# Summing the messages over destinations: loads of four columns, eight split slots, one-hots on GpSimd

## The chip, the cores and the metric

The kernel runs on one core of a Trainium2 chip. A core has TensorE (matrix products, into PSUM), VectorE (DVE), ScalarE (ACT), GpSimd (POOL) and SyncE (SP), which here issues most of the DMAs. The engines run side by side and wait for one another through semaphores. The metric is the device time of one execution in microseconds (us), as the median of several runs; lower is better.

## The reference

A stack of graph layers on 1250 nodes with 768 features and 20000 edges sorted by destination: two GCN layers, a relational layer (34 relations) with a GCN behind it, two attention layers and one more GCN, each block with a layer norm and a residual. The change touches the end of the relational layer:

```python
seg = edge_type * n + dst
agg = jax.ops.segment_sum(x[src], seg, num_segments=N_REL * n)
cnt = jax.ops.segment_sum(ones, seg, num_segments=N_REL * n)
mean = agg.reshape(N_REL, n, -1) / jnp.maximum(cnt, 1.0).reshape(N_REL, n, 1)
h1 = jnp.einsum('rni,rio->no', mean, W_rel) + x @ W_root + b_rgcn
xw = h1 @ W_gcn
```

`dst` is int(1250 u²) for uniform u, so the first nodes have many more edges than the last ones.

## The kernel before

The kernel computes the mean over relations edge by edge. In the relation stage each edge's source row, multiplied by its relation's weights and by the reciprocal of its count, is scattered by GpSimd to `messages` in DRAM, in the order of the edges, which is the order of destinations. 128 edges make a column: there are 157, padded to 160.

The stage after it, which the program calls the sum, computes h1 for ten tiles of 128 nodes. For a tile, TensorE turns its rows of h (six transposes, `turn`, L1240) and multiplies them by the root weights (36 matmuls, `products`, L1249), into two PSUM banks. On top of that it adds the tile's columns of messages: a column is multiplied by a one-hot matrix (edge to node of the tile), 128 x 128, made by VectorE at L1205 from the edge's destination. Columns go in groups of four, `QUAD`; a column at a border of tiles is taken for both.

Products are split for accuracy: a float32 operand is written as a rounded high part and a low rest. So a column passes through four engines. SP loads it into one of four slots `w_raw[:, b]` (L502) as soon as VectorE is done with that slot (`Q.ylow`). ScalarE copies it to the high part, `y_part[:, 0, k]` in the memory of `xw` (L817), when the load has landed and TensorE is done with this slot of the group before (`Q.ymm`). VectorE makes the one-hot (L1205) and subtracts the high part from the message for the low part (L1207). TensorE multiplies the high and the low part, each in two halves of 384 features: four matmuls (L1417).

The order of each engine's instructions is written out by hand in `sum_tile` of each engine. VectorE: copy the next tile's rows (L1199), all columns of this tile, the low parts of the next tile's turned rows (`turn_low`, L856), then, when TensorE is done with the tile's last column, the bias and PSUM into `h_act` (L1212). ScalarE: the columns, then the high parts of the next tile's turned rows (L808). TensorE: the next tile's turning, the root products of this tile, its columns. SP: the columns' loads. The bounds of the loops are read from small tables (`bounds`, L358 and L359; `quads`, L361 to L364), since they depend on the data.

GpSimd issues the gathers and scatters of the relation stage (L599, L604, L636), each behind a small copy of its addresses (L595, L630), and has nothing to do in the sum. Before the relation stage it reads back the edge records (L590) and starts the first gathers, for which VectorE waits at L1166.

Semaphores `pre.*` order the preparation at the start of the kernel, in which the unused rows of `messages` are zeroed as well (L400 to L405).

Of the kernel before, what the change touches and what calls it, by code (L numbers as in the profile page):

```python
# [5 lines left out]
P = 128  # L6
# [8 lines left out]
ds = bass.ds  # L15
# [5 lines left out]
QUAD = 4  # L21
RING = 4

class EdgeSems:

    def __init__(self, sem):
# [6 lines left out]
        self.turned = sem("pre_turned")  # L35
        self.extremes = sem("pre_extremes")
        self.extremes_turned = sem("pre_extremes_turned")
        self.best = sem("pre_best")
        self.row = sem("pre_row")
        self.tot = sem("pre_tot")  # L40
        self.prefix = sem("pre_prefix")
# [58 lines left out]
class SumSems:  # L100

    def __init__(self, sem):
        self.copied = sem("sum_copied")
        self.turned = sem("sum_turned")
        self.high = sem("sum_high")
        self.low = sem("sum_low")
        self.mm = sem("sum_mm")
        self.yhigh = sem("sum_yhigh")
        self.ylow = sem("sum_ylow")  # L110
        self.ymm = sem("sum_ymm")
        self.ofree = sem("sum_ofree")
# [47 lines left out]
def gnn_stack(nc, A, out):  # L160
# [33 lines left out]
    messages = nc.dram_tensor("messages", (YROWS, D), F32).ap()  # L194
    inv_table = nc.dram_tensor("inv_table", (NP * NR, 1), F32).ap()

    with ExitStack() as ctx:
# [11 lines left out]
        w_raw = sb("w_raw", [P, KB, D], F32)  # L209
        agg_w = sb("agg_w", [P, 2, NT, P], F32R)[:]  # L210
        h_t = sb("h_t", [P, 2, KB, P], F32R)
        rows = sb("rows", [P, 4, D], F32)
# [34 lines left out]
        y_part = xw[:, :, 0:QUAD, 0:D]  # L247
        h_flat = h_act[:].rearrange("p t d -> p (t d)")
        rows_flat = rows[:].rearrange("p a d -> p (a d)")
        raw_flat = w_raw[:].rearrange("p k d -> p (k d)")  # L250
        n_eq = NR * ECP
        rec_in = rows_flat[:, D:D + 3 * RIN].bitcast(I32).rearrange("p (c w) -> p c w", w=3)
# [6 lines left out]
        oh = h_flat[:, n_eq:n_eq + ohw].bitcast(BF16).rearrange("p (u n) -> p u n", u=2)  # L259
        adj_t = rows_flat[:, 0:NP]  # L260
# [60 lines left out]
        x_copy, zeroed = sem("x_copy"), sem("zeroed")  # L321
# [17 lines left out]
        y_land = [sem(f"y_land{b}") for b in range(QUAD)]  # L339
# [6 lines left out]
        QMAX = NT * (ECP // QUAD)  # L346
# [32 lines left out]

        def score_row(t, which):  # L380

            return ps_flat[:, ds(t % 2 * (6 * 512) + which * 512, P)]
# [3 lines left out]
        def _(sp):  # L386
# [10 lines left out]
            sp.dma_start(x_state[0:N, :], x).then_inc(x_copy, 16)  # L397
            sp.wait_ge(pre.zeros, 1)
            sp.dma_start(x_state[N:NP, :], zero_rows[0:NP - N, 0, :]).then_inc(zeroed, 16)
            at = E  # L400
            while at < ECP * P:
                n = min(ECP * P - at, 3 * 80)
                sp.dma_start(messages[at:at + n, :].rearrange("(p r) d -> p r d", r=3), zero_rows[0:n // 3, :, :])\
                  .then_inc(zeroed, 16)
                at += n  # L405
# [60 lines left out]
            sp.wait_ge(x_copy, 16)  # L466
            sp.wait_ge(zeroed, 16 * 3)
# [65 lines left out]
        def _(pool):  # L533
# [111 lines left out]
            pool.sem_inc(R.stored, 1)  # L645

        @block.scalar
        def _(act):
# [185 lines left out]
        def _(dve):  # L835
# [178 lines left out]
            dve.wait_ge(pre.turned, 1)  # L1014
# [13 lines left out]
            dve.sem_inc(pre.extremes, 1)  # L1028
            dve.wait_ge(pre.extremes_turned, 1)
# [419 lines left out]
```

## Time and profile before

| | |
|---|---|
| time, median of 3 runs | 3085.62 us (3083.73 to 3091.12) |
| profiled execution, its own time | 3085.96 us |
| its span in the trace | 3084.0 us |
| mean granted TensorE clock | 0.939 |
| busy: PE, DVE, ACT, POOL | 85%, 52%, 37%, 28% |

The time of an execution is its span and about 2 us around it. In the profile, idle time stands with what ended it ("releaser"), and the busy time of TensorE is that of a pipeline whose ends are modelled. PEclk is the granted clock, 1.00 for 2.4 GHz and 0.50 for 1.2 GHz.

### The profile page before, as it was taken

How to read it: one execution, taken by the hardware profiler on the slowest of the kernel's cores; microseconds unless marked ns; L12 is line 12 of the kernel's file. 1: busy time of each engine (PE TensorE's matmuls, PEld its weight loads, DVE VectorE, ACT ScalarE, POOL GpSimd, SP SyncE). 2: the span in 40 equal slices, each digit the busy share in tenths (PEclk: the TensorE clock that was granted, in tenths of full speed). 3: DMA queues.
4: the chain of work that ended last, by engine and by line, in shares of the span. 5: the costliest groups of instructions: out<-in, count | busy, mean ns of one | idle time of the engine just before them, and what ended most of it. 6: DMA issues, size and time to landing. Idle time of an engine off the chain costs nothing.

```text
span 3084.0 us, 52263 instructions
## 1 busy us (share of the span) xinstructions
PE 2621.4 (85%) x14502; PEld 2425.3 (79%) x14503; DVE 1604.0 (52%) x3028; ACT 1126.3 (37%) x1925; POOL 859.8 (28%) x1207
## 2 busy tenths in 40 slices
PE   0666388976999999999999999677778898987899
PEld 0222188976999999999999999556668887987799
DVE  7765543354344333443334433477764577577734
ACT  0011323232444444444444444355433235446521
POOL 1666610002555555555555555100000000000000
PEclk9987689998999999999999999889989998998999
DMA  3000110124445544555544554577660201001102
GB/s 108 1 1 1 44 47 0 45 86 169 175 174 182 196 174 174 174 188 190 174 174 172 195 188 143 184 239 228 207 199 21 77 25 36 10 13 69 51 21 91
DMA packets 116601, 358.08 MB, mean 116 GB/s; under 512 B 23709, under 2 KB 24177, under 8 KB 116337
## 3 DMA queue, kind: packets, MB, share of 16 engines
q1 hardware_dynamic: 78097, 220.40, 21.2%
q0 software_dynamic: 38464, 137.17, 12.8%
q8 instruction: 23, 0.38, 0.0%
q14 instruction: 17, 0.14, 0.0%
HBM read 267.97 MB, written 93.37 MB: 117 GB/s over the span
## 4 chain that ended last, share of the span: by engine, by line
PE 72%; DVE 11%; issue 5%; ACT 5%; DMA 4%; DVEq 2%; POOL 0%; ACTq 0%; SPq 0%; POOLq 0%
PE ps L1249 50%; PE ps L1304 12%; PE ps L1240 5%; PE ps L1356 4%; DMA w_raw<-messages 3%; DVE xw L1207 1%; PE ps L1417 1%; ACT xw L817 1%; DVE h_act L1115 1%; ACT rows L721 1%; DVE h_act L927 1%; DVEq L1113 1%; PE ps L1362 1%; DVE w_a L850 1%; DVE rows L981 1%
## 5 line engine op out<-in xcount | busy, mean ns | idle before, releaser
L1249 PE MATMUL ps<-w_a,h_t 128*128 128x384 f32 x5580 | 1032.3, 342 | 2.4 <-DVE h_t L856 2.1
L1249 PEld LDWEIGHTS ps<-w_a,h_t 128*128 128x128 f32 x5580 | 982.3, 192 | 6.9 <-DVE h_t L856 4.6
L1304 PE MATMUL ps<-xw,agg_w 128*128 128x384 f32 x2800 | 524.5, 350 | 78.8 <-DVE agg_w L952 47.2
L1304 PEld LDWEIGHTS ps<-xw,agg_w 128*128 128x128 f32 x2800 | 512.6, 197 | 87.7 <-issue 77.1
L1249 PE MATMUL ps<-xw,h_t 128*128 128x384 f32 x3132 | 577.4, 341 | 0.0
L1155 DVE TENSOR_TENSOR h_t<-ps,h_t 128x256 fp32r<-128x256 f32 x516 | 218.7, 424 | 678.5 <-ACT h_t L784 482.3
L1249 PEld LDWEIGHTS ps<-xw,h_t 128*128 128x128 f32 x3132 | 549.0, 188 | 0.0
L784 ACT ACTIVATE h_t<-ps 128x256 fp32r<-128x256 f32 x516 | 198.2, 384 | 677.2 <-PE ps L1249 472.0
L1240 PE MATMUL ps<-ident,rows 128*128 128x128 f32 x1458 | 206.8, 280 | 129.7 <-DVE rows L863 71.2
L636 POOL DMA_INDIRECT messages<-rows,rec_stage x172 | 199.9, 1162 | 354.1 <-ACT rows L778 354.1
L1240 PEld LDWEIGHTS ps<-ident,rows 128*128 128x128 f32 x1458 | 176.4, 144 | 146.3 <-issue 86.1
L599 POOL DMA_INDIRECT h_act<-h_table,rec_stage x175 | 188.7, 1078 | 147.1 <-POOL rec_stage L595 119.4
L1417 PE MATMUL ps<-xw,agg_w 128*128 128x384 f32 x736 | 178.2, 381 | 54.5 <-DVE xw L1207 50.0
L817 ACT ACTIVATE xw<-w_raw 128x768 fp32r<-128x768 f32 x184 | 152.6, 843 | 167.3 <-DMA w_raw<-messages 91.2
L1417 PEld LDWEIGHTS ps<-xw,agg_w 128*128 128x128 f32 x736 | 134.7, 206 | 95.9 <-DVE xw L1207 94.5
L1356 PE MATMUL ps<-h_act 128*128 128x512 bf16 x552 | 151.0, 393 | 63.1 <-DVE h_act L1115 53.6
L604 POOL DMA_INDIRECT w_at<-inv_table,rec_stage x175 | 182.9, 1045 | 61.4 <-issue 61.4
L1207 DVE TENSOR_TENSOR xw<-w_raw,xw 128x768 fp32r<-128x768 f32 x184 | 176.0, 957 | 44.4 <-ACT xw L817 43.7
L575 POOL DMA_INDIRECT records<-rec_stage x157 | 158.4, 1009 | 128.4 <-POOL rec_stage L571 121.7
L856 DVE TENSOR_TENSOR h_t<-ps,h_t 128x256 fp32r<-128x256 f32 x213 | 86.9, 423 | 185.6 <-ACT h_t L664 184.2
L1356 PEld LDWEIGHTS ps<-h_act 128*128 128x128 bf16 x552 | 43.4, 105 | 173.8 <-DVE h_act L1115 133.2
L664 ACT ACTIVATE h_t<-ps 128x256 fp32r<-128x256 f32 x183 | 70.2, 385 | 295.8 <-PE ps L1249 206.1
(183 smaller groups left out, 2188.8 us busy)
## 6 DMA issues: line engine op xcount, KB each, us to landing
w_raw<-in_L_gnn_W_rel SPq DMA_DIRECT2D x68, 1152.0 KB
w_raw<-messages SPq DMA_DIRECT2D x184, 384.0 KB, 3.8
rows<-x_state SPq DMA_DIRECT2D x50, 384.0 KB, 3.0
w_raw<-in_L_gnn_W SPq DMA_DIRECT2D x10, 1152.0 KB
x_state<-rows SPq DMA_DIRECT2D x30, 384.0 KB, 2.3
h_table<-h_act SPq DMA_DIRECT2D x10, 384.0 KB, 2.4
x_state<-in_x SPq DMA_DIRECT2D x1, 3750.0 KB, 14.2
out<-rows SPq DMA_DIRECT2D x9, 384.0 KB
```

What stands on the lines that cost most here:

```text
L599: pool.indirect_dma_start(out=x_ring[:, k, :], out_offset=None, in_=h_table, in_offset=bass.IndirectOffsetOnAxis(gather_at[:, k, 0:1], 0)) ...
L604: pool.indirect_dma_start(out=w_at[:, k:k + 1], out_offset=None, in_=inv_table, in_offset=bass.IndirectOffsetOnAxis(gather_at[:, k, 1:2], ...
L636: pool.indirect_dma_start(out=messages, out_offset=bass.IndirectOffsetOnAxis(scatter_at[:, k, :], 0), in_=rows[:, 2 + u, :], in_offset=Non ...
L784: act.activation(h_t[:, 0, 2 * g:2 * g + 2, :], turn_group(g).rearrange("p (k n) -> p k n", k=2), ACT.Copy)\
L817: act.activation(y_part[:, 0, k, :], w_raw[:, k, :], ACT.Copy).then_inc(Q.yhigh, 1)
L1155: dve.tensor_tensor(h_t[:, 1, 2 * g:2 * g + 2, :], turn_group(g).rearrange("p (k n) -> p k n", k=2), h_t[:, 0, 2 * g:2 * g + 2, :].bitcast ...
L1207: dve.tensor_tensor(y_part[:, 1, k, :], w_raw[:, k, :], y_part[:, 0, k, :].bitcast(F32), ALU.subtract)\
L1240: ins = pe.transpose(turn_out(k), tile[:, k * P:(k + 1) * P], ident[:])
L1249: ins = pe.matmul(acc(h), h_t[:, a, k, :], w[:, b, k, h * HF:(h + 1) * HF], start=(k == 0 and a == 0 and b == 0), stop=(stop and k == KB - ...
L1304: ins = pe.matmul(ps[:, 2 + 2 * u + h, 0:wide], agg_w[:, a, b, :], xw[:, c, b, h * HF:h * HF + wide], start=first, stop=last, skip_group_c ...
L1356: ins = pe.matmul(ps_flat[:, lo:hi], oh[:, k % 2, 0:P], oh[:, k % 2, P + lo:P + hi], start=False, stop=True, skip_group_check=True)
L1417: ins = pe.matmul(rel_acc(t)(h), agg_w[:, 0, k, :], y_part[:, b, k, h * HF:(h + 1) * HF], start=False, stop=True, skip_group_check=True)
```

## The change

- The message slots grow from four to eight. `w_raw` (six rows of 768) and `rows` (four) become parts of one memory, `land`; its first eight rows are the ring for the loads. One DMA of 1536 KB brings a whole group of four columns, and two groups can be under way.
- SP loops over pairs of groups. The first column of each group comes from a new table, `quad_col`, that VectorE computes in `quad_columns` once, before the relation stage. A group's load is issued when VectorE has split the group two before it. Then SP waits until the group before the new one has landed and counts `Q.yready` up, for which ScalarE waits.
- The slots of the split parts grow from four to eight (`LAND`). Their addresses, and those of the ring, now depend on the group's number.
- The one-hots are made by GpSimd, in four slots as before: for every tile a copy of 128 node numbers, for every column a copy of the column's destinations, and the comparison.
- The turned rows go through `rows[:, 2]` in place of `rows[:, 0]`.
- Several semaphores of the preparation are put together, and the zeroing of `messages` is laid out differently.

```diff
-            with sp.Fori(0, NT) as t:
-                q0, q1, c0 = quads(sp, t)
-                with sp.Fori(q0, q1) as q:
-                    for b in range(QUAD):
-                        j = column(c0, q, q0, b)
-                        sp.wait_ge(Q.ylow, q * QUAD + b + 1)
-                        sp.dma_start(w_raw[:, b, :], messages[ds(j * P, P), :])\
-                          .then_inc(y_land[b], 16)
+            pairs = sp.value_load(ctl_half[0:1, 1:2], min_val=1, max_val=QMAX // 2)
+            with sp.Fori(0, pairs) as i:
+                for u in range(2):
+                    j = sp.value_load(quad_col[0:1, ds(2 * i + u, 1)], min_val=0, max_val=ECP - QUAD)
+                    sp.wait_ge(Q.ylow, i * LAND + (QUAD * u + QUAD))
+                    sp.dma_start(y_ring[:, QUAD * u:QUAD * (u + 1), :], message_rows[:, ds(j, QUAD), :]).then_inc(y_land[u], 16)
+                    sp.wait_ge(y_land[1 - u], i * 16 + 16 * u)
+                    sp.sem_inc(Q.yready, 1)
+            sp.wait_ge(y_land[1], pairs * 16)
+            sp.sem_inc(Q.yready, 1)
...
+            with pool.Fori(0, NT) as t:
+                q0, q1, c0 = quads(pool, t)
+                pool.wait_ge(Q.hot, q0 * QUAD)
+                pool.tensor_copy(hot_iota, iota_n[:, ds(t * P, P)]).then_inc(pre.rec_copy, 1)
+                with pool.Fori(q0, q1) as q:
+                    for k in range(QUAD):
+                        j = column(c0, q, q0, k)
+                        pool.tensor_copy(hot_node[:, k:k + 1], edge[:, 1, ds(j, 1)]).then_inc(pre.rec_copy, 1)
+                        pool.wait_ge(Q.ymm, q * QUAD + (k + 1 + QUAD))
+                        pool.sem_inc(turn_taken, 1)
+                        pool.wait_ge(pre.rec_copy, q * QUAD + t + (EC + k + 2))
+                        pool.sem_inc(turn_taken, 1)
+                        pool.tensor_scalar(agg_w[:, 0, k, :], hot_iota, hot_node[:, k:k + 1], None, ALU.is_equal)\
+                            .then_inc(Q.hot, 1)
...
-                        act.wait_ge(y_land[k], q * 16 + 16)
+                        act.wait_ge(Q.yready, q + 2)
                         act.wait_ge(Q.ymm, q * QUAD + (k + 1))
-                        act.activation(y_part[:, 0, k, :], w_raw[:, k, :], ACT.Copy).then_inc(Q.yhigh, 1)
+                        act.activation(part(0, q, k), landed(q, k), ACT.Copy).then_inc(Q.yhigh, 1)
...
+            def quad_columns():
+
+                q_first, q_base, q_delta = att[0:1, 0, :], att[0:1, 1, :], seg_max[0:1, 0, :]
+                dve.wait_ge(R.addr, 1)
...
+                for t in range(NT):
+                    link(dve.tensor_scalar(quad_step, iota_n[0:1, 0:QMAX], q_first[:, t:t + 1], q_delta[:, t:t + 1],
+                                           ALU.is_ge, ALU.mult))
+                    link(dve.tensor_tensor(quad_acc, quad_acc, quad_step, ALU.add))
...
-                        dve.wait_ge(Q.ymm, q * QUAD + (k + 1))
-                        dve.tensor_scalar(agg_w[:, 0, k, :], iota_n[:, ds(t * P, P)], edge[:, 1, ds(j, 1)], None, ALU.is_equal)
                         dve.wait_ge(Q.yhigh, q * QUAD + (k + 1))
-                        dve.tensor_tensor(y_part[:, 1, k, :], w_raw[:, k, :], y_part[:, 0, k, :].bitcast(F32), ALU.subtract)\
+                        dve.tensor_tensor(part(1, q, k), landed(q, k), part(0, q, k).bitcast(F32), ALU.subtract)\
                            .then_inc(Q.ylow, 1)
...
                     for k in range(QUAD):
-                        pe.wait_ge(Q.ylow, q * QUAD + (k + 1 + QUAD))
+                        pe.wait_ge(Q.hot, q * QUAD + (k + 1))
+                        pe.wait_ge(Q.ylow, q * QUAD + (k + 1 + LAND))
                         for b in range(2):
                             for h in range(2):
-                                ins = pe.matmul(rel_acc(t)(h), agg_w[:, 0, k, :], y_part[:, b, k, h * HF:(h + 1) * HF],
+                                ins = pe.matmul(rel_acc(t)(h), agg_w[:, 0, k, :], part(b, q, k)[:, h * HF:(h + 1) * HF],
                                                 start=False, stop=True, skip_group_check=True)
```

`part(a, q, k)` and `landed(q, k)` are the slots `q % 2 * QUAD + k` of `y_part` and of the ring; `link` makes VectorE wait for its own last instruction.

## Rows read from the trace of the kernel before

**Rows 1.** TensorE's message matmuls by tile: stretch, us, PE busy (xcount), PEclk, DMA share, GB/s

```profile
1967.00:2052.70 85.70, 54.38 (x208) 0.87 0.75 238
2052.70:2094.50 41.80, 23.31 (x96) 0.92 0.71 221
...
2130.00:2158.90 28.90, 15.52 (x64) 0.94 0.70 227
...
2188.30:2210.00 21.70, 10.54 (x48) 1.00 0.65 219
...
2231.80:2256.50 24.70, 11.35 (x48) 0.85 0.64 204
2256.50:2282.30 25.80, 12.22 (x48) 0.76 0.58 178
2282.30:2296.10 13.80, 6.66 (x32) 0.96 0.40 128
sum 329.10, PE 178.24; mean PE 17.82
```

**Rows 2.** Groups of instructions in the sum, 1965 to 2297 us

```profile
L1207 DVE TENSOR_TENSOR xw<-w_raw,xw 128x768 fp32r<-128x768 f32 x184 | 176.0, 957 | 44.4 <-ACT xw L817 43.7
L817 ACT ACTIVATE xw<-w_raw 128x768 fp32r<-128x768 f32 x184 | 152.6, 843 | 167.3 <-DMA w_raw<-messages 91.2 <-PE ps L1417 70.8 <-issue 1.9
...
L1205 DVE TENSOR_SCALAR agg_w<-iota_n,edge 128x128 fp32r x176 | 49.7, 282 | 46.6 <-PE ps L1417 29.8 <-issue 16.8
```

**Rows 3.** The chain of waits inside tile 0: start us, us, what

```profile
2015.28 3.83 DMA w_raw<-messages
2019.21 0.85 ACT xw L817
2020.09 0.97 DVE xw L1207
...
2039.50 4.42 DMA w_raw<-messages
```

**Rows 4.** Timeline behind the sum: two loads of 1152 KB, and ScalarE waiting

```profile
2297.08 0.92 SPq L411 DMA_DIRECT2D w_raw<-in_L_gnn_W_gcn  x2
...
2302.50 2.12 ACT L655 ACTIVATE w_a<-w_raw 128x2304 fp32r<-128x2304 f32 x1 [8.63 <-DMA w_raw<-in_L_gnn_W_gcn]
...
2305.38 2.12 ACT L655 ACTIVATE w_a<-w_raw 128x2304 fp32r<-128x2304 f32 x1 [0.75 <-DMA w_raw<-in_L_gnn_W_gcn]
```

**Rows 5.** Timeline at the border of tiles 2 and 3

```profile
2126.70 0.96 DVE L1207 TENSOR_TENSOR xw<-w_raw,xw 128x768 fp32r<-128x768 f32 x1
...
2129.04 0.96 DVE L1212 TENSOR_TENSOR h_act<-ps,rows 128x768 f32 x1 [0.37 <-PE ps L1417]
...
2131.15 6.49 PE L1249 MATMUL ps<-w_a,h_t 128*128 128x384 f32 x36
2132.29 0.29 DVE L1205 TENSOR_SCALAR agg_w<-iota_n,edge 128x128 fp32r x1 [1.83 <-issue]
```

**Rows 6.** Register instructions of ScalarE at L778: ns min/median/max, first and last start

```profile
L778 ACTq FUSED_REGOPS  x344: 98/100/141, 752.9 to 1947.0; - x172
```

**Rows 7.** GpSimd's first instruction that waits for its own engine

```profile
6.17 0.29 POOL L554 TENSOR_SCALAR_AFFINE_SELECT ident<-ident 128x128 f32<-128x128 f32 x1 [0.16 <-POOL rows L551]
```

**Rows 8.** GpSimd and VectorE by line, ns min/median/max, over the whole kernel

```profile
L595 POOL COPY rec_stage<-rows x175: 185/190/934, 732.9 to 1944.3; 128x2 int32 x172, 128x2 int32<-128x2 int32 x3
...
L636 POOL DMA_INDIRECT messages<-rows,rec_stage x172: 1014/1014/1770, 755.1 to 1949.0; - x172
...
L1163 DVE TENSOR_TENSOR xw<-w_raw,xw x102: 946/956/1035, 749.3 to 1872.8; 128x768 fp32r<-128x768 f32 x102
...
L1114 DVE TENSOR_SCALAR h_act<-iota_n,edge x184: 539/549/789, 77.2 to 349.3; 128x1280 bf16<-128x1280 uint16 x184
```

**Rows 9.** Timeline ahead of the relation stage

```profile
725.89 0.11 POOL L589 MEMSET rows<- 128x10 int32 x1 [320.95 <-DMA h_table<-h_act]
...
740.90 0.56 DVE L1167 COPY rows<-h_act 128x768 f32<-128x768 f32 x1 [18.50 <-POOLq L612]
```

More of the change, by code:

```diff
@@ L21 @@
 QUAD = 4
+LAND = 2 * QUAD
 RING = 4
@@ L34, in __init__ @@
         self.floats = sem("pre_floats")
[L35 to L41, printed above, removed]
+        self.pe_step = sem("pre_pe_step")
+        self.dve_step = sem("pre_dve_step")
         self.tile_ctl = sem("pre_tile_ctl")
@@ L108, in __init__ @@
         self.mm = sem("sum_mm")
+        self.yready = sem("sum_yready")
+        self.hot = sem("sum_hot")
         self.yhigh = sem("sum_yhigh")
@@ L208, in gnn_stack @@
         w_a = sb("w_a", [P, 2, KB, D], F32R)
-        w_raw = sb("w_raw", [P, KB, D], F32)
+        land = sb("land", [P, KB + 4, D], F32)
+        w_raw, rows = land[:, 0:KB, :], land[:, KB:KB + 4, :]
+        y_ring = land[:, 0:LAND, :]
         agg_w = sb("agg_w", [P, 2, NT, P], F32R)[:]
         h_t = sb("h_t", [P, 2, KB, P], F32R)
-        rows = sb("rows", [P, 4, D], F32)
         bias = rows[:, 3, :]
@@ L338, in gnn_stack @@
         Q = SumSems(sem)
-        y_land = [sem(f"y_land{b}") for b in range(QUAD)]
+        y_land = [sem(f"y_land{b}") for b in range(2)]
         block = ctx.enter_context(nc.Block())
@@ L378, in tile_rows, with landed, part @@
             return ap[:, ds(t, 1), :].rearrange("p a d -> p (a d)")
+        def landed(q, k):
+            return y_ring[:, ds(q % 2 * QUAD + k, 1), :].rearrange("p a d -> p (a d)")
+        def part(a, q, k):
+            return y_part[:, a, ds(q % 2 * QUAD + k, 1), :].rearrange("p a d -> p (a d)")
         def score_row(t, which):
@@ L1027, in _ @@
                 link(ins)
-            dve.sem_inc(pre.extremes, 1)
-            dve.wait_ge(pre.extremes_turned, 1)
-            dve.tensor_reduce(small[0:2 * NT, 1, 0:1], ps[0:2 * NT, 2, 0:P], AX.X, ALU.max).then_inc(pre.best, 1)
-            dve.wait_ge(pre.row, 1)
+            dve.sem_inc(pre.dve_step, 1)
+            dve.wait_ge(pre.pe_step, 2)
+            dve.tensor_reduce(small[0:2 * NT, 1, 0:1], ps[0:2 * NT, 2, 0:P], AX.X, ALU.max).then_inc(pre.dve_step, 1)
+            dve.wait_ge(pre.pe_step, 3)
             up, down = ps[0:1, 3, 0:NT], ps[0:1, 3, NT:2 * NT]
@@ L1165, in rel_split @@
                         ins.then_inc(w_low, 1)
+            quad_columns()
             dve.wait_ge(R.ready, 1)
@@ L1190, in _ @@
             dve.sem_inc(Q.ofree, 2)
-            dve.sem_inc(Q.ylow, QUAD)
+            dve.sem_inc(Q.ylow, LAND)
             dve.wait_ge(R.h_back, 16)
-            dve.tensor_copy(rows[:, 0, :], tile_rows(h_act, 0)).then_inc(Q.copied, 1)
+            dve.tensor_copy(rows[:, 2, :], tile_rows(h_act, 0)).then_inc(Q.copied, 1)
             turn_low(Q, 0)
@@ L1328, in _ @@
                 ins = pe.transpose(ps[:, 1, a * 32:(a + 1) * 32], float_b[:, a, :], ident[0:32, 0:32])
-            ins.then_inc(pre.turned, 1)
-            pe.wait_ge(pre.extremes, 1)
-            pe.transpose(ps[0:2 * NT, 2, 0:P], small[:, 0, 0:2 * NT], ident[:]).then_inc(pre.extremes_turned, 1)
-            pe.wait_ge(pre.best, 1)
+            ins.then_inc(pre.pe_step, 1)
+            pe.wait_ge(pre.dve_step, 1)
+            pe.transpose(ps[0:2 * NT, 2, 0:P], small[:, 0, 0:2 * NT], ident[:]).then_inc(pre.pe_step, 1)
+            pe.wait_ge(pre.dve_step, 2)
             pe.matmul(ps[0:1, 3, 0:2 * NT], small[0:2 * NT, 1, 0:1], ident[0:2 * NT, 0:2 * NT], start=True, stop=True)\
-              .then_inc(pre.row, 1)
-            pe.wait_ge(pre.tot, 1)
+              .then_inc(pre.pe_step, 1)
+            pe.wait_ge(pre.dve_step, 3)
             own = small[:, 3, 0:NR]
             pe.matmul(ps[:, 4, 0:NR], before[:], own, start=True, stop=True, skip_group_check=True)
-            pe.matmul(ps[:, 4, 64:64 + NR], ones[:], own, start=True, stop=True, skip_group_check=True).then_inc(pre.prefix, 1)
+            pe.matmul(ps[:, 4, 64:64 + NR], ones[:], own, start=True, stop=True, skip_group_check=True).then_inc(pre.pe_step, 1)
             cuts = [(0, 512), (512, 1024), (1024, NP + NR)]
@@ L1397, in _ @@
             pe.wait_ge(w_low, 2 * (w_no["root"] + 1))
-            pe.sem_inc(Q.ymm, QUAD)
+            pe.sem_inc(Q.ymm, LAND)
             pe.wait_ge(Q.copied, 1)
-            turn(Q, rows[:, 0, :])
+            turn(Q, rows[:, 2, :])
             def sum_tile(t, more):
@@ L1405, in sum_tile @@
                     pe.wait_ge(Q.copied, t + 2)
-                    turn(Q, rows[:, 0, :])
+                    turn(Q, rows[:, 2, :])
                 pe.wait_ge(Q.ofree, t + 1)
```

55 lines of the change are left out of this document (33 added, 22 removed).

## The prediction

> **What bounds the kernel now.** I read the page's slices first (the sum lies near 2000 to 2300 us), then the busy time by tile, then the groups of the stage, then the chain of waits, then single borders in the timeline. The sum takes 329.1 us for ten tiles [rows 1]. Sixteen matmuls are a group of four columns, so the tiles have 13, 6, 5, 4, 4, 3, 3, 3, 3 and 2 groups, 46 in all. TensorE's message matmuls are busy for 178 of these 329 us, VectorE's subtractions for 176, ScalarE's copies for 153: no engine fills the stage. ScalarE waits 91 us for loads and 71 us for TensorE [rows 2], and VectorE in turn for ScalarE.
>
> The chain says why. Inside a tile it goes round: load 3.8 us, ScalarE's copy 0.85, VectorE's subtraction 0.97, and 0.25 until the slot's next load starts. Between 2015.28 and 2039.50 there are four such rounds, 6.05 us each, one per group [rows 3]. Four loads are in flight, and what limits is the time from free slot to filled slot, not the bytes. Between tiles a second limit shows: from VectorE's last subtraction (end at 2127.66) it takes 1.4 us to the bias addition, 3.5 to the root products, which last 6.5, and 4.6 to VectorE's next one-hot [rows 5]. During the products only four columns can be split ahead; then ScalarE stands still until TensorE frees a slot, and the loads behind it too. Tiles with three groups took 21.7 us at full clock [rows 1], which is 3.5 us over three rounds.
>
> **The change part by part.** The sum is made against the profiled execution, 3085.96 us (span 3084.0 and 1.96 around it), 0.3 above the median of the runs.
>
> *The load of a group.* No message load of 1536 KB is in the trace, and I take its time from the two weight loads of 1152 KB: issued at 2297.08 and within 0.9 us, the first landed at about 2302.4 and the second at about 2305.3, where ScalarE began [rows 4]. So 1152 KB cost 2.9 us more, and 2.4 us are fixed: 1536 KB land in 2.4 + 3.9 = 6.3 us. I take 6.05 to 6.3. The ends: 5.3 us, the time of the 1152 KB, and 7.2, if the other group still has a fifth of its bytes to move (0.9 us).
>
> *The new round.* A slot's group is issued 0.25 us after its predecessor is drained, lands 6.05 later, waits 0.1 for SP, and is then split: first copy 0.85, four subtractions of which three start 0.9 apart and the last takes 0.96, 3.65 in all [rows 2, 3]. New register work for the ring's addresses stands between the wait and the instruction on both engines; two such instructions took 0.1 us each in the one place that has them [rows 6], so 0.2 on ScalarE and 0.2 on VectorE (ends 0 and 0.3 each). Sum 11.3 us for two groups, 5.65 a group. There is a second loop: SP counts a group ready only after it has issued the next load, and for that waits until VectorE has drained the group before. So ScalarE can't start a group while VectorE still splits the last one. That loop is 0.25 + 0.45 (issue) + 0.2 (two signals) + 0.2 + 0.85 + 0.2 + 3.65 = 5.8 us a group. The longer one holds: 5.8 against 6.05. Without the register work it would be 5.4. Thus inside long tiles the doubled ring brings only 0.25 us a group, since it buys depth and gives most of it back by coarse signals.
>
> *The border of tiles.* Here the change helps more. After the last subtraction VectorE goes through the low parts, bias, copy and the reading of its bounds as before; one bound less and no one-hot bring its first subtraction from 4.8 (0.2 behind the one-hot) to about 4.0 us after the drain [rows 5]. Then one group ends at 7.8 us and each further one 5.8 later: T(n) = 2.0 + 5.8 n, while root products run beside the first two. For n = 3 that is 19.4 against 21.7, for n = 4 25.2 against 28.9, for n = 6 36.8 against 41.8 [rows 1]. Over tiles 1 to 9, 33 groups: 18 + 191.4 = 209.4, and 0.9 less since the last ends in the bias addition, against 243.4: 34.9 us. Of these, 7.1 lie in the two tiles of 24.7 and 25.8 us, whose granted clock was 0.85 and 0.76 [rows 1]; I leave them to the clock, so 27.8. Tile 0: first subtraction 0.6 earlier, twelve rounds 0.2 shorter, 2.9 us.
>
> *The one-hots.* 184 instructions of 0.282 us, 52 us, leave VectorE [rows 2]; most lay in its waits for ScalarE, and the part on the path is in T(n). That hides behind 5.8 in the steady rounds. It doesn't quite after the root products: only four one-hots exist, the fifth can start when TensorE frees the first at 10.8 us, and the last of n groups is ready at 11.1 + 1.4 (4n - 5). For n = 3 with its column on TensorE 21.6 us, against 20.4 by the splits. About 1 us for each of nine tiles: 9 us lost.
>
> *Smaller ones.* TensorE's matmuls now take their address from a register. In the steady rounds TensorE has time; behind the root products, where eight columns wait, a tenth of a us per column costs 0.8 us a tile at most: 2 us (0 to 8). `quad_columns` is some 20 linked instructions on 400 elements, between 0.28 (128 elements) and 0.96 (768) each, so 0.5, and ten small ones: 10 + 2 to 14 us. It starts when GpSimd's memset is done at 726.0, and VectorE is needed at 740.9 [rows 9]: covered by 15 us, with little to spare. But GpSimd's address copies and gathers beside it can be held by up to 0.75 us each, and the relation stage starts behind them. 2 us (0 to 6). The merged semaphores, the zeroing and the moved rows: same work, in places where other loads or waits cover it; 0.
>
> *Sum.* 27.8 + 2.9 - 9 - 2 - 2 = 17.7 us less: 3085.96 - 17.7 = 3068.
>
> The shared port is where a rule speaks against this change. The holds above are GpSimd behind VectorE. The Trainium skill, "SBUF — State Buffer", section "SBUF: two separate sides", says that VectorE and GpSimd share a port pair by an exclusive lock, which an instruction of GpSimd or one of VectorE with two SBUF inputs holds to its end while the other is blocked fully; each subtraction is of that kind. By that rule, the trace agrees on the one side (0.19 to 0.93), and shows less on the other: subtractions of the relation stage went from 0.956 to 1.035 at most.
>
> **The rivals.**
>
> *B, GpSimd and VectorE take turns, slower.* Place: columns within a group. If every GpSimd instruction that meets a subtraction also delays the next one, a group grows. The row for it is VectorE's comparison beside GpSimd's copies, 0.549 in the median and up to 0.789 [rows 8], 0.2 to 0.24 longer; against it stands the 1.035. Four such delays a group are 0.8 us: rounds of 6.6 instead of 5.8, 36 us on 45 rounds, so 3068 + 36 = 3104. The same follows from a slow column on GpSimd alone: a tile can't be shorter than 11 + 4c(n - 1), ten tiles 110 + 144c. That reaches 329 us at c = 1.53; with one full hold of 0.75 a column, c = 1.65, it is 348, and with the 2 of `quad_columns` the kernel takes about 3107. It decides from c = 1.53, close above my 1.4.
>
> *C, the border is worth all that it seems.* c near 1, the clock stays up since TensorE's gaps are shorter, no register cost: 9 + 7 + 2 come back, and 0.2 us on each of 45 rounds, 9: 3068 - 27 = 3041. For it: tiles at clock 1.00 were 3 to 4 us shorter. Against: nothing in the trace shows address registers at no cost.
>
> *D, the coarse load eats the gain.* The group lands 7.2 us after its issue, and the first loop is 12.4 us, 6.2 a group: 0.4 more on 45 rounds, 18 us, 3068 + 18 = 3086, no change. The change would then do what it says and bring nothing, being bound by landing as now.
>
> **How the numbers follow.** My forecast 0.46, B 0.21, C 0.20, D 0.13. The range goes from somewhat below C to B: lower end, full removal of all uncertain costs with the load at 5.3 us, about 3038; upper 3104. The likeliest case has 3058 to 3078 for its own. A difference of 0.3% is 9.3 us, about what a measurement tells from no change: faster below 3076.4. Faster: most of my case (0.42) and C (0.20), 0.62. Same: the rest of mine and most of D, 0.15. Slower: B and a little of D, 0.23.
>
> **What would show it.** In the profile after: the sum at some 310 us, the chain inside tile 0 through ScalarE, VectorE's four subtractions and SP, with no or little landing time, rounds of 5.8; ScalarE's idle time ended by SP and not by TensorE; tiles of three groups near 20 to 21 us; TensorE waiting now and then for GpSimd's comparison, which takes about 0.3 us alone and up to 1 us behind a subtraction. The subtractions stay at 0.96. VectorE's first copy of the relation stage at 741 to 744. The forecast is wrong if subtractions grow to 1.1 or more, if TensorE mostly waits for GpSimd (B), if the load's landing ends ScalarE's waits in every group (D), or if the sum falls below 290 (C).

## The result, and the profile after

| | before | after |
|---|---|---|
| median | 3085.19 us (20 runs, 3080.15 to 3094.67) | 3091.03 us (20 runs, 3086.18 to 3099.54) |
| profiled execution, its own time | 3085.96 | 3087.34 |
| its span; granted clock | 3084.0; 0.939 | 3085.6; 0.936 |
| the sum, ten tiles | 329.1 | 325.4 |

The ratio of after to before is 1.0017, with a 95% interval of 1.0009 to 1.0025: some 5 us slower, a small loss, but clear of 1 (the medians themselves lie 5.8 us apart). All ratios here are of fast executions, without one of the kernel before of 3244.61 us and one of 5266.12 us of the kernel with fine loads and four copies. Forecast were 3068 us and a sum of some 309 (329.1 less 27.8 and 2.9, plus 9 and 2). The sum gave back 3.7 us instead of 20.

TensorE's message matmuls by tile (stretch, us, PE busy, PEclk, DMA share, GB/s), for tiles 0, 1, 3 and 5, against [rows 1]:

```profile
1971.30:2056.20 84.90, 54.03 (x208) 0.85 0.75 257
2056.20:2096.80 40.60, 23.87 (x96) 0.92 0.66 225
...
2131.70:2160.90 29.20, 14.97 (x64) 0.88 0.64 219
...
2189.70:2213.50 23.80, 10.99 (x48) 0.86 0.57 201
```

Tile 0 and tile 1 are about 1 us shorter (85.7 and 41.8 before), the tile of four groups is as long as it was (28.9), and the two tiles of three groups that had taken 21.7 and 21.8 grew to 23.8. The two later ones, which had a low clock before (24.7 and 25.8 us at 0.85 and 0.76), took 23.4 and 22.0 at 0.93. The groups of the sum, 1965 to 2297 us (busy, mean ns, idle time and what ended it), against [rows 2]:

```profile
L1461 PE MATMUL ps<-xw,agg_w 128*128 x736 | 180.3, 392 | 54.4 <-POOL agg_w L670 54.2 <-issue 0.2
L670 POOL TENSOR_SCALAR agg_w<-rec_out 128x128 fp32r<-128x128 uint16 x182 | 170.8, 939 | 79.7 <-PE ps L1461 44.0 <-POOL rec_out L665 35.7
L1250 DVE TENSOR_TENSOR xw<-land,xw x184 | 168.9, 979 | 92.6 <-ACT xw L843 83.3 <-issue 9.4
...
L843 ACT ACTIVATE xw<-land x184 | 140.2, 833 | 169.7 <-SPq L512 143.3 <-PE ps L1461 23.1 <-SPq L514 3.2
...
L665 POOL COPY rec_out<-edge 128x1 f32 x181 | 69.1, 382 | 0.5
```

Read the idle columns. The loads no longer end ScalarE's waits (91.2 us before), nor does TensorE much (70.8 before, 23.1 now); SP's signal L512 does. TensorE's own idle time is still 54 us, but now all of it ends in GpSimd's comparison L670, where 50 of 54.5 us ended in VectorE's subtractions in the kernel before:

```profile
L1417 PE MATMUL ps<-xw,agg_w 128*128 128x384 f32 x736 | 178.2, 381 | 54.5 <-DVE xw L1207 50.0
```

It shows most at the end of a tile. From VectorE's last subtraction to the bias addition it was 1.1 to 2.4 us in the ten tiles before, 16.9 in all; now it is 4.3 to 5.7, 50.9 in all, since TensorE still waits for one-hots. VectorE's wait for TensorE ahead of the bias addition (us, times, longest), before and after:

```profile
DVE h_act L1212 <- PE ps L1417: 7.6, 10, 1.4
...
DVE h_act L1255 <- PE ps L1461: 41.9, 10, 4.7
```

So the sum without these stretches did get shorter, by some 38 us (3.7 and 34), as much as the 34.9 and 2.9 that the forecast had for the borders and for tile 0 at whatever clock, and TensorE's wait for one-hots took almost all of it. GpSimd's and VectorE's instructions by line (ns min/median/max, first and last start), and from the same view of L510 the landing of a group's load:

```profile
L670 POOL TENSOR_SCALAR agg_w<-rec_out x184: 602/605/2092, 1962.5 to 2294.8; 128x128 fp32r<-128x128 uint16 x184
...
L665 POOL COPY rec_out<-edge x184: 180/186/989, 1961.8 to 2294.4; 128x1 f32 x184
...
L1250 DVE TENSOR_TENSOR xw<-land,xw x184: 943/955/1085, 1973.9 to 2291.3; - x184
...
DMA to landing us min/median/max: 6.3/6.5/10.4
```

The comparison takes 0.605 us by itself and 0.94 in the mean, the copy 0.186 and 0.38. VectorE's subtractions beside them have a median of 0.955, as before, a mean of 0.979 (0.957 before), and never more than 1.085. One group in the timeline (start, us, engine and line, idle time before):

```profile
2009.94 3.66 DVE L1250 TENSOR_TENSOR xw<-land,xw  x4 [2.33 <-ACT xw L843]
...
2010.30 1.86 POOL L670 TENSOR_SCALAR agg_w<-rec_out 128x128 fp32r<-128x128 uint16 x1 [0.20 <-POOL rec_out L665]
2012.11 0.67 POOL L665 COPY rec_out<-edge 128x1 f32 x1
...
2012.98 1.09 POOL L670 TENSOR_SCALAR agg_w<-rec_out 128x128 fp32r<-128x128 uint16 x1 [0.20 <-POOL rec_out L665]
...
2014.03 0.18 POOL L665 COPY rec_out<-edge 128x1 f32 x1
...
2014.41 0.60 POOL L670 TENSOR_SCALAR agg_w<-rec_out 128x128 fp32r<-128x128 uint16 x1 [0.20 <-POOL rec_out L665]
...
2015.35 0.60 POOL L670 TENSOR_SCALAR agg_w<-rec_out 128x128 fp32r<-128x128 uint16 x1 [0.20 <-POOL rec_out L665]
```

VectorE's four subtractions fill 2009.94 to 2013.60. GpSimd's instructions that start ahead of their end take 1.86, 0.67 and 1.09 us; those behind it 0.18 and 0.60. Undisturbed, a column costs GpSimd 2015.35 less 2014.41, 0.94 us: 0.60 for the comparison, 0.18 for the copy, 0.20 for the wait, less a slight overlap. The chain of waits inside tile 0 is GpSimd's as well (start, us, what):

```profile
2018.91 0.68 POOL rec_out L665
...
2025.13 0.68 POOL rec_out L665
...
2031.13 0.68 POOL rec_out L665
...
2037.21 0.68 POOL rec_out L665
```

The same held copy comes back every 6.1 us, one round of four columns, where [rows 3] had a round of 6.05 through load, ScalarE and VectorE. TensorE's bound has moved to another engine, and the round is as long as before. VectorE's own rounds beside it, which hang on SP's signal, are 6.05 us in the mean of tile 0, so the two are nearly equal inside a tile, and GpSimd's lag comes out at the tile's end.

### The profile page after: what moved, and what is told of

Read it like the earlier page. It is cut to its first block, busy times and chain, and to the rows that moved or that the text cites. A ratio compares the mean times of both kernels' runs of the same rounds, so it can differ in the third digit from the quotient of the medians.

```text
span 3085.6 us, 54594 instructions
## 1 busy us (share of the span) xinstructions
PE 2620.4 (85%) x14502; PEld 2431.2 (79%) x14503; DVE 1577.5 (51%) x2874; ACT 1114.0 (36%) x1925; POOL 1097.6 (36%) x1586
## 4 chain that ended last, share of the span: by engine, by line
PE 72%; DVE 10%; issue 8%; ACT 4%; POOL 3%; DVEq 2%; DMA 1%; POOLq 1%; ACTq 0%; SPq 0%
PE ps L1292 48%; PE ps L1347 11%; PE ps L1283 5%; PE ps L1399 4%; PE ps L1461 2%; POOL rec_out L665 1%; POOL agg_w L670 1%; DVE h_act L1141 1%; DVE h_act L953 1%; ACT land L747 1%; DVEq L1139 1%; PE ps L1405 1%; DVE w_a L876 1%; DVE land L1007 1%; DVE land L966 1%
## 5 line engine op out<-in xcount | busy, mean ns | idle before, releaser
L1347 PE MATMUL ps<-xw,agg_w 128*128 128x384 f32 x2800 | 526.2, 350 | 78.1 <-DVE agg_w L978 46.7
L1347 PEld LDWEIGHTS ps<-xw,agg_w 128*128 128x128 f32 x2800 | 514.0, 197 | 87.3 <-issue 77.6
L810 ACT ACTIVATE h_t<-ps 128x256 fp32r<-128x256 f32 x516 | 198.3, 384 | 675.9 <-PE ps L1292 477.5
L647 POOL DMA_INDIRECT messages<-land,rec_stage x172 | 200.1, 1163 | 353.2 <-ACT land L804 353.2
L1283 PE MATMUL ps<-ident,land 128*128 128x128 f32 x1458 | 207.2, 280 | 133.5 <-DVE land L889 71.5
L1283 PEld LDWEIGHTS ps<-ident,land 128*128 128x128 f32 x1458 | 176.7, 144 | 150.2 <-issue 89.6
L1461 PE MATMUL ps<-xw,agg_w 128*128 x736 | 180.3, 392 | 54.4 <-POOL agg_w L670 54.2
L1250 DVE TENSOR_TENSOR xw<-land,xw x184 | 168.9, 979 | 92.6 <-ACT xw L843 83.3
L1461 PEld LDWEIGHTS ps<-xw,agg_w 128*128 128x128 f32 x736 | 144.5, 217 | 88.5 <-issue 88.3
L843 ACT ACTIVATE xw<-land x184 | 140.2, 833 | 169.7 <-SPq L512 143.3
L670 POOL TENSOR_SCALAR agg_w<-rec_out 128x128 fp32r<-128x128 uint16 x184 | 172.0, 935 | 80.5 <-PE ps L1461 44.0
```

The costliest lines, as they stand in the source:

```text
L647: pool.indirect_dma_start(out=messages, out_offset=bass.IndirectOffsetOnAxis(scatter_at[:, k, :], 0), in_=rows[:, 2 + u, :], in_offset=Non ...
L670: pool.tensor_scalar(agg_w[:, 0, k, :], hot_iota, hot_node[:, k:k + 1], None, ALU.is_equal)\
L810: act.activation(h_t[:, 0, 2 * g:2 * g + 2, :], turn_group(g).rearrange("p (k n) -> p k n", k=2), ACT.Copy)\
L1250: dve.tensor_tensor(part(1, q, k), landed(q, k), part(0, q, k).bitcast(F32), ALU.subtract)\
L1283: ins = pe.transpose(turn_out(k), tile[:, k * P:(k + 1) * P], ident[:])
L1347: ins = pe.matmul(ps[:, 2 + 2 * u + h, 0:wide], agg_w[:, a, b, :], xw[:, c, b, h * HF:h * HF + wide], start=first, stop=last, skip_group_c ...
```

## The experiments

In this section "the sum" is the time from VectorE's first copy of the next tile's rows to its last bias addition: 329.1 us before, 325.4 after. The rounds are those of tile 0.

**One half of the change at a time.** First the new ring, slots and loads, with the one-hots back on VectorE (against the change):

```diff
-            with pool.Fori(0, NT) as t:
...
+                        dve.wait_ge(Q.ymm, q * QUAD + (k + 1 + QUAD))
+                        dve.tensor_scalar(agg_w[:, 0, k, :], iota_n[:, ds(t * P, P)], edge[:, 1, ds(j, 1)], None, ALU.is_equal)
```

> The loads, the ring and the eight split slots of the change, with the one-hots on VectorE again, one ahead of each subtraction. Theory A (GpSimd's 1.52 us a column bounds the changed kernel): GpSimd is out, but three one-hots a group now lie between subtractions in the loop VectorE, SP, ScalarE (5.8 us a group), so 6.4 to 6.6 us a group, and only four columns get ahead of the root products: sum about 335 us (325 to 345), kernel about 3095. Rival R1 (the signals over SP bound the changed kernel, GpSimd just keeps pace): the same loop made longer, also 335. Rival R2 (the ring is worth the 25 us that was forecast, and only GpSimd's one-hots ate it): sum about 305, kernel about 3068.

Measured: 3091.3 us, ratio 1.0028 [1.0018, 1.0038], sum 336.3, rounds 6.35 and 6.38 in turn. ScalarE again waits for SP's signal (by group, as above):

```profile
L1237 DVE TENSOR_TENSOR xw<-land,xw x184 | 175.5, 954 | 55.2 <-ACT xw L827 52.4 <-issue 0.2
...
L827 ACT ACTIVATE xw<-land x184 | 140.2, 832 | 184.8 <-SPq L511 132.3 <-PE ps L1447 48.2 <-SPq L513 4.3
```

This is the forecast's second loop with the one-hots in it, as expected: the ring alone is slower than the four single slots. A part of the 7 us of sum can be the clock, granted at 0.85 in this kernel's sum and at 0.90 in before's. Then the other half, the old loads and slots with GpSimd's one-hots (against the kernel before; there is no `quad_columns` in it):

```diff
+                        pool.tensor_scalar(agg_w[:, 0, k, :], hot_iota, hot_node[:, k:k + 1], None, ALU.is_equal)\
+                            .then_inc(Q.hot, 1)
...
-                        dve.tensor_scalar(agg_w[:, 0, k, :], iota_n[:, ds(t * P, P)], edge[:, 1, ds(j, 1)], None, ALU.is_equal)
```

> The four loads of one column, four message slots and four split slots of the kernel before, with the one-hots on GpSimd. Theory A: GpSimd's column cycle bounds again, 11 + 4c(n-1) a tile with c near 1.5: sum 320 to 330 us, VectorE waits less for anything else, kernel within 5 us of before. R1 and R2 (GpSimd isn't the bound): VectorE loses 0.28 us a column from its part of the round, sum about 310, kernel about 3070.

Measured: 3102.02 us, 1.0062 [1.0046, 1.0079], sum 340.0, worse than either account had it. GpSimd's work costs the same with the old loads:

```profile
L667 POOL TENSOR_SCALAR agg_w<-rec_out 128x128 fp32r<-128x128 uint16 x184 | 168.2, 914 | 80.5 <-PE ps L1457 44.9 <-POOL rec_out L662 35.6
...
L662 POOL COPY rec_out<-edge 128x1 f32 x184 | 87.4, 475 | 0.6
```

Each half alone costs 7 to 11 us of sum, and together they give 4. I read this as each half hiding a part of what the other costs; what makes the second half as slow as 340 wasn't taken apart.

**A shorter GpSimd column.** One copy of four node numbers for a group in place of four copies; all else is the change:

```diff
+                    pool.tensor_copy(hot_node, edge[:, 1, ds(j, QUAD)]).then_inc(pre.rec_copy, 1)
                     for k in range(QUAD):
-                        pool.tensor_copy(hot_node[:, k:k + 1], edge[:, 1, ds(j, 1)]).then_inc(pre.rec_copy, 1)
```

> The changed kernel with one copy of a group's four node numbers on GpSimd in place of four copies. Theory A: three of four copies with their waits and holds go, 0.45 us a column, c falls from 1.52 to about 1.07, and the next bound is the loop over SP, 5.8 us a group: sum about 303 us (295 to 312), kernel about 3070. R1: sum stays at 325, GpSimd gets idle time instead. R2: as A.

Measured: 3070.32 us, 0.9953 [0.9937, 0.997], sum 306.0, rounds 5.80 to 6.18, 5.97 in the mean. GpSimd now waits 96 us for TensorE, where it waited 44:

```profile
L672 POOL TENSOR_SCALAR agg_w<-rec_out 128x128 fp32r<-128x128 uint16 x184 | 181.0, 998 | 103.7 <-PE ps L1463 96.5 <-POOL rec_out L666 7.1
...
L666 POOL COPY rec_out<-edge 128x4 f32 x46 | 12.5, 271 | 10.7 <-POOL agg_w L672 9.8
```

A cheaper column alone brings the kernel to within 3 us of the forecast time, and the tiles to 21.2 to 22.6 us for three groups (the first three of them) and 26.7 for four. The rounds of VectorE fell by under 0.1 us; most of the 19 us were won at the ends of tiles, where the bias addition now waits 25.0 us for TensorE in all, against 41.9. So it is the column's cost that kept the change from its forecast.

**The hold itself.** VectorE's subtraction takes its second input from PSUM (a bank of zeros) in place of the high part in SBUF. The low part is then the whole message, so this kernel doesn't compute the reference; the instruction has the same size and the same time, 0.95 us.

```diff
-                        dve.tensor_tensor(part(1, q, k), landed(q, k), part(0, q, k).bitcast(F32), ALU.subtract)\
+                        dve.tensor_tensor(halves(part(1, q, k)), halves(landed(q, k)),
+                                          ps[:, 7, 0:HF].unsqueeze(1).broadcast_to([P, 2, HF]), ALU.subtract)\
```

> The changed kernel with the second input of VectorE's message subtraction taken from a PSUM bank of zeros in place of the high part in SBUF; so the low part is the whole message, and the output isn't the reference's. Same length of instruction expected, 0.96 us. Theory A with the hold by VectorE's two SBUF inputs: GpSimd's comparisons stay at 0.61 us and copies at 0.19, c is 0.94, the loop over SP bounds: sum about 305, kernel about 3072. If holds come from any VectorE instruction: comparisons stay at 0.94 in the mean, sum 325. R1: comparisons get short but the sum stays 325.

Measured: 3048.57 us, 0.988 [0.9863, 0.9896], sum 292.3.

```profile
L1251 DVE TENSOR_TENSOR xw<-land,ps 128x768 f32 x184 | 163.2, 950 | 92.6 <-ACT xw L843 91.5 <-issue 1.0
...
L670 POOL TENSOR_SCALAR agg_w<-rec_out 128x128 fp32r<-128x128 uint16 x184 | 111.8, 608 | 143.1 <-PE ps L1463 113.9 <-POOL rec_out L665 29.2
...
L665 POOL COPY rec_out<-edge 128x1 f32 x184 | 34.8, 189 | 0.6
```

The comparison falls from 0.94 to 0.61 us in the mean and the copy from 0.38 to 0.19, with VectorE as busy as before. The hold is thus a matter of the second SBUF input, and it costs 0.33 + 0.19 = 0.52 us a column and 33 us of sum. My expectation had the mechanism and too small a gain. The Trainium skill, "SBUF — State Buffer", section "SBUF: two separate sides", has a VectorE instruction with two SBUF inputs and a GpSimd instruction that reads SBUF exclude each other, the later one blocked fully. By that rule, the trace agrees for GpSimd; for VectorE it differs, whose subtractions took 0.979 us in the mean beside GpSimd's held comparisons and 0.950 here.

**The loop over SP's signals.** The kernel with one copy again, and ScalarE waiting for the landings itself instead of for SP's count (against the kernel with one copy):

```diff
-                     sp.wait_ge(y_land[1 - u], i * 16 + 16 * u)
-                     sp.sem_inc(Q.yready, 1)
...
-                        act.wait_ge(Q.yready, q + 2)
+                        act.wait_ge(y_land[0], (q + 2) // 2 * 16 + 1)
+                        act.wait_ge(y_land[1], (q + 1) // 2 * 16 + 1)
```

> The kernel of e3_one_copy, with ScalarE waiting for the two landing semaphores itself; SP only issues loads, and nothing is signalled by way of it. If the loop VectorE, SP, ScalarE sets the rounds of 6.0 us in e3 (as the prediction had it), they fall to the landing loop, (0.25 + 6.6 + 0.1 + 0.2 + 0.85 + 0.2 + 3.65) / 2 = 5.9 us, and only ScalarE's first copy moves under VectorE's last subtractions: sum 300 us against 306. If GpSimd is still close to the bound, sum 303 to 306. Kernel 3064 to 3070.

Measured: 3066.71 us, 0.9946 [0.9929, 0.9964], sum 300.9. Rounds go in pairs at first, 3.75 and 8.25, so 12.0 for two; over tile 0 the mean round is 6.08. The chain shows what holds now:

```profile
2003.60 6.57 DMA land<-messages
...
2015.54 6.65 DMA land<-messages
...
2027.77 6.95 DMA land<-messages
```

With the signals gone the first loop of the forecast appears, over the group's landing: 6.0 to 6.1 us a group where I had worked out 5.65. The rounds are no shorter than with the signals, so the two loops are equally long within what this shows, and the times (0.9946 and 0.9953) can't be told apart; the 5 us of sum lie outside tile 0. The first three tiles of three groups take 19.8 to 20.4 us and those of four 28.3 and 24.5.

**Finer loads.** One load a column into eight slots, issued as each slot is drained, on top of the kernel above:

```diff
-                    sp.wait_ge(Q.ylow, i * LAND + (QUAD * u + QUAD))
-                    sp.dma_start(y_ring[:, QUAD * u:QUAD * (u + 1), :], message_rows[:, ds(j, QUAD), :]).then_inc(y_land[u], 16)
+                    for b in range(QUAD):
+                        sp.wait_ge(Q.ylow, i * LAND + (QUAD * u + b + 1))
+                        sp.dma_start(y_ring[:, QUAD * u + b, :], messages[ds(j * P + b * P, P), :])\
+                          .then_inc(y_land[QUAD * u + b], 16)
```

> The kernel of e5_direct with the group's load cut into four loads of one column, each issued when its own slot of the eight is free and each with its own semaphore. If the coarseness of the load (6.5 us to land, four columns at once) gives back the ring's depth, rounds fall from 6.0 to what GpSimd (4c with c 1.07 to 1.3) or VectorE (4 x 0.9 and registers) allow, 4.3 to 5.2 us: sum 265 to 285, kernel 3030 to 3050. If GpSimd's held one-hots bound already, rounds stay near 6, sum 300, kernel 3066.

Measured: 3054.6 us, 0.991 [0.9883, 0.9937], sum 289.9, a little more than I expected, with a mean round near 5.1. GpSimd is back in the chain (share of the stretch 1990 to 2040 us by line):

```profile
by line: POOL agg_w L673 39.3%; issue 28.0%; PE ps L1465 24.4%; POOL rec_out L667 5.3%; POOLq L663 1.5%; POOLq L669 0.9%; POOLq L667 0.9%; POOLq L672 0.7%; POOLq L670 0.3%; POOLq L666 0.2%; POOLq L671 0.1%
```

The same with `quad_columns` behind the relation stage:

```diff
-            quad_columns()
...
+            quad_columns()
             dve.wait_ge(bias_land, 16 * (BIAS_ORDER.index("sum") + 1))
```

> e6_fine_loads with quad_columns computed behind the relation stage, where VectorE waits for the last scatters, in place of ahead of it. If quad_columns costs what the interval from GpSimd's memset to the first row copy shows (15.8 to 16.8 us against 15.0), the kernel is 1 to 2 us below e6; if its DMA descriptors were held by more than that, 4 us below; the interval is 15.0 again either way.

Measured: 3050.8 us, 0.988 [0.986, 0.99], sum 290.0. From GpSimd's memset to VectorE's first row copy it took 15.8 us, where I expected the 15.0 of [rows 9]. This interval doesn't follow the table: it was 15.7 to 16.8 in the kernels with the early one, 16.0 in the kernel with the old loads, which has none, and with the late one 15.8 in this kernel and in the last one below and 15.0 in the two with the one-hots on VectorE. The median is 3.8 us below that of the kernel before it, but the profiled execution 1.6 above, and the two intervals of the ratio overlap. So the price of the early table isn't shown. And the fine loads with the change's four copies a group kept (against the first kernel with fine loads, so with the early table):

```diff
-                    pool.tensor_copy(hot_node, edge[:, 1, ds(j, QUAD)]).then_inc(pre.rec_copy, 1)
...
+                        pool.tensor_copy(hot_node[:, k:k + 1], edge[:, 1, ds(j, 1)]).then_inc(pre.rec_copy, 1)
```

> The changed kernel with loads of one column into its eight slots and ScalarE waiting for them directly, but GpSimd's four copies a group kept. Theory A (GpSimd's column cycle bounds the changed kernel): finer loads bring nothing while GpSimd takes 1.5 us a column, and since VectorE is busier it may be held more: sum 320 to 330, kernel 3085 to 3092. If the coarse load were a bound of its own beside it: sum 300.

Measured: 3085.43 us, 0.9999 [0.9988, 1.0011], sum 316.7.

```profile
L671 POOL TENSOR_SCALAR agg_w<-rec_out 128x128 fp32r<-128x128 uint16 x184 | 177.3, 963 | 66.2 <-POOL rec_out L666 35.5 <-PE ps L1463 30.7
```

Better loads without a cheaper column bring the kernel to where it was before the change, with 9 us of sum less than the change has (I had expected 320 to 330); the cheaper column on top of them takes another 31 us. So relief on the other side helps a little, and three times as much lies in GpSimd's column.

**GpSimd left out.** The fine loads and the late table, with the one-hots on VectorE one ahead of each subtraction:

```diff
-                        pool.tensor_scalar(agg_w[:, 0, k, :], hot_iota, hot_node[:, k:k + 1], None, ALU.is_equal)\
...
+                        dve.tensor_scalar(agg_w[:, 0, k, :], iota_n[:, ds(t * P, P)], edge[:, 1, ds(j, 1)], None, ALU.is_equal)
```

> e7_fine_late with the one-hots on VectorE again, one ahead of each subtraction as in the kernel before; GpSimd does nothing in the sum. VectorE takes 4 x (0.9 + 0.28) = 4.7 us a group and nothing holds anything, but only four columns get ahead of the root products. Tiles of 3.5 + 4.9 n: 35 + 225, and some 10 for stretches at the low clock: sum 270 us (260 to 280), kernel 3032. If the move of the one-hots to GpSimd were worth its 52 us of VectorE time, this must be slower than e7 (290): 295 or more.

Measured: 3029.18 us, 0.983 [0.9813, 0.9846], sum 270.0, rounds 4.26: the fastest kernel here that computes the reference, 53 us below before's 3082.07 in the same comparison. In tile 0 VectorE is hardly ever without work (timeline):

```profile
1995.89 0.30 DVE L1237 TENSOR_SCALAR agg_w<-iota_n,edge 128x128 fp32r x1
1996.08 0.97 DVE L1239 TENSOR_TENSOR xw<-land,xw  x1
...
1996.95 0.30 DVE L1237 TENSOR_SCALAR agg_w<-iota_n,edge 128x128 fp32r x1
1997.15 0.97 DVE L1239 TENSOR_TENSOR xw<-land,xw  x1
```

A one-hot and a subtraction take 1.06 us together here, where subtractions alone start 0.9 us apart: the one-hot that the change removed costs VectorE less than 0.2 us, against 0.94 to 1.5 on GpSimd. The same with the four one-hots of a group behind its four subtractions:

```diff
+                    for k in range(QUAD):
...
+                        dve.tensor_scalar(agg_w[:, 0, k, :], iota_n[:, ds(t * P, P)], edge[:, 1, ds(j, 1)], None, ALU.is_equal)\
+                           .then_inc(Q.hot, 1)
```

> As e9_fine_vector, but a group's four one-hots stand behind its four subtractions, so that eight columns can be split ahead of the root products' end, at the price that TensorE gets a tile's last four columns only after the one-hots: about 2 us less ahead of the columns and 3 us more behind them. Sum 270 to 285, no better than e9.

Measured: 3033.11 us, 0.9848 [0.9828, 0.9869], sum 271.8. The place of the one-hots within a group can't be told apart by these runs.

**Fine loads without the hold.** The kernel with fine loads, one copy and late table, its subtraction's second input from PSUM as above (again not the reference's result):

```diff
-                        dve.tensor_tensor(part(1, q, k), landed(q, k), part(0, q, k).bitcast(F32), ALU.subtract)\
+                        dve.tensor_tensor(halves(part(1, q, k)), halves(landed(q, k)),
+                                          ps[:, 7, 0:HF].unsqueeze(1).broadcast_to([P, 2, HF]), ALU.subtract)\
```

> e7_fine_late with VectorE's second input from a PSUM bank of zeros, as in e4; the low part is the whole message, so the output isn't the reference's. If the shared port is what bounds e7, GpSimd's comparisons are 0.61 us again and a group takes 4 us or a little over: sum 255 to 270, kernel 3025. If it is TensorE with its root products and the low clock, 280 to 290.

Measured: 2990.72 us, 0.9702 [0.9684, 0.9719], sum 237.9, less than expected.

```profile
L1467 PE MATMUL ps<-xw,agg_w 128*128 x736 | 143.7, 347 | 4.2 <-DVE xw L1255 2.4 <-POOL agg_w L674 1.4 <-issue 0.2
...
L674 POOL TENSOR_SCALAR agg_w<-rec_out 128x128 fp32r<-128x128 uint16 x184 | 112.3, 621 | 95.5 <-PE ps L1467 85.3 <-POOL rec_out L668 7.2 <-issue 0.4
```

In its message matmuls TensorE hardly waits any more, 4.2 us. Between this kernel and the one with its SBUF input (sum 290.0) the only difference is the subtraction's second input: 52 us. Some of them are the clock, which rose with it, 0.97 granted in this kernel's sum against 0.93. So offloading the one-hots is a good idea in itself, 238 us against 270 with them on VectorE, and it is the hold that makes it a loss, 290. Whether a correct kernel can avoid it (a subtraction that reads its high part from PSUM, say) wasn't tried.

## Why the prediction was wrong

**The failed step is the cost of GpSimd's column and the 9 us set down for what it doesn't hide**, "I take 0.5 of hold per column: c = 1.4, 5.6 us a group. That hides behind 5.8 in the steady rounds", and behind the root products "About 1 us for each of nine tiles: 9 us lost". The parts of the column measured:

| | forecast | measured |
|---|---|---|
| copy alone, its wait | 0.19, 0.16 | 0.186, 0.20 |
| comparison alone | 0.29 | 0.605 |
| registers and signals | 0.25 | none on top |
| hold | 0.5 | 0.52 |
| c | 1.4 | 1.46, and 1.52 in the rounds of tile 0 |

The comparison was priced by the select of the same size [rows 7] at less than half of what it takes; the 0.25 for registers, of which nothing shows in the column's 0.94 us, made up for most of it by luck. So c was off by only 0.06 to 0.12. But it stood beside the point where it decides, and I treated 5.6 against 5.8 as hidden. Above all I priced the shortfall in tiles of three groups at about 1 us, 20.4 with it, where they took 23.8. My own formula for rival B, 11 + 4c(n - 1) for a tile, gives with c = 1.5 tiles of 41, 35, 29 and 23 us for six to three groups; measured were 40.6, 34.9, 29.2 and 23.8. Summed, 110 + 144c is 326 us against 325.4; some of that agreement is luck, since it gives 83 us for tile 0, which took 84.9, and 17 for the last tile, which took 14.0. The formula was in the text, with its crossing at 1.53, and the sum of the forecast should have been made with it: at c = 1.4 it gives 312, already more than my 309, and each 0.1 more costs 14 us. In the terms of the sum: without the 9 us my forecast has 300, and 325 were measured, so the term was about 25 us in place of 9, by an estimate that leaves the other terms as they were. The next largest miss in it is tile 0, for which I took 2.9 us off and 0.8 came off (the text has 0.25 us a round in one place and 0.2 in another).

The other steps:

- *The load of a group*, 6.3 us: 6.3 at least and 6.5 in the median in the change. Right; rival D's 7.2 wasn't the median of any kernel (6.7 at most, with direct waits).
- *The two loops*, 5.65 and 5.8 us a group: the signal loop shows with one copy (rounds near 6.0), the landing loop with direct waits (6.0). Both stand, 0.2 and 0.4 short. In the change itself both lie just under GpSimd's 6.1. That ScalarE's idle time would end in SP's signal was right (143 us).
- *The border*, T(n) = 2.0 + 5.8 n, 19.4, 25.2 and 36.8 us: with direct waits and one copy tiles of 19.8 to 20.4, 24.5 and 28.3, and 39.4. Near for three groups, short for one tile of four and for six.
- *`quad_columns`*, 2 us: not shown, as above. The 20 linked instructions took 0.47 to 0.56 us each (0.5 forecast) and were done 3.7 us ahead of the first row copy.
- *TensorE's address registers*, 2 us: not measured apart.

**The rivals.** B had 0.21, and its second form happened: the slow column on GpSimd, with TensorE waiting for it. Its first form didn't: the subtractions stayed at 0.955 in the median and 0.979 in the mean (at most 1.085), so VectorE is hardly held in turn. Its price was 348 us of sum for a full hold of 0.75 a column; with 0.52 it is 326. C asked for a column near 1 us, a sum of 282 (27 below the forecast's 309): the kernel with the PSUM input has such a column, 0.61 + 0.19 + 0.20, and 292.3; its terms for clock and registers weren't measured apart. D gave the right time, 3086, by a mechanism that isn't there in the change: SP waited only 15.6 us for landings in the whole sum. A loop over the landing close to its 6.2 us a group shows only in the kernel with direct waits (6.08).

**What stays open.** The forecast missed by 23 us. 16 of them are the sum, 3 the rest of the profiled execution, which grew by 5 with 2 foreseen, and 3.7 the distance of the median after from its profiled run. The 5 are 1.8 ahead of the relation stage, less 0.4 before it,

```profile
725.44 0.11 POOL L600 MEMSET land<- 128x10 int32 x1 [319.54 <-DMA h_table<-h_act]
...
742.24 0.56 DVE L1213 COPY land<-h_act 128x768 f32<-128x768 f32 x1 [3.75 <-POOLq L623]
```

(16.8 us from the one to the other, 15.0 in [rows 9]), some 3 in the relation stage and the load of `h_act` behind it (1226.1 against 1223.2 us), and 1 behind the sum. The relation stage's stretch varied from 1220 to 1227 us between experiments in which its code was the same, so its 3 us can't be given a cause. Time outside the sum, profiled time less sum, is 2756 to 2760 us in before and the three kernels without GpSimd's one-hots, and 2761 to 2763 in those with them (2772 with fine loads and four copies), with the PSUM input too. Why isn't known.

## What to carry to other kernels

Before work moves to an idle engine, price its instruction on that engine, not by another operation of the same size: the comparison took 0.605 us on GpSimd and under 0.2 of VectorE's time. Write the bound of the new engine as a formula over each stretch (here 11 + 4c(n - 1) a tile) and take the larger of the two bounds there; a cover of 0.2 us in 5.8 is none when c is uncertain by 0.3. And ask which resource limits before deepening a buffer: eight slots filled by coarse loads brought nothing (ring alone, 1.0028); the same slots filled one by one, with ScalarE waiting for each landing itself (and the table computed later), brought 53 us.

## What the runs showed of the hardware

- GpSimd's short instructions are held beside VectorE subtractions with two SBUF inputs, for longer than the end of the one under way: a comparison of 0.605 us took 1.86 in the group shown, and up to 2.09 elsewhere, though a subtraction lasts 0.96. With one input in PSUM the mean is 0.608.
- The hold goes nearly one way. VectorE's subtractions had a mean of 0.966 to 0.979 us beside GpSimd's comparisons and 0.950 to 0.957 without them or with the PSUM input; the longest took 1.122.
- A wait of GpSimd for its own last instruction took 0.20 us.
- A load of 1536 KB landed 6.5 to 6.7 us after its issue in the median (6.2 at least, 10.5 at most); a single column of 384 KB took 3.8 before, and 4.4 to 5.3 with eight slots.
